# Eigenvalues by bisection: two counting passes and a straight line in place of the third pass

## The reference

```python
deg = jnp.sum(A, axis=0) + jnp.sum(A, axis=1) - jnp.diagonal(A)
d_inv_sqrt = jnp.where(deg > 0, jax.lax.rsqrt(deg), 0.0)
L_norm = d_inv_sqrt[:, None] * (jnp.diag(deg) - A) * d_inv_sqrt[None, :]
_, U = jnp.linalg.eigh(L_norm)
agg = jnp.einsum('mn,bnd->bmd', U.T, features)
h = jax.nn.relu(agg @ W1 + b1)
out = jnp.einsum('nm,bmd->bnd', U, h @ W2 + b2)
```

## Time and profile before

| | us |
|---|---|
| median of 3 runs (1450.54 to 1452.41) | 1451.95 |
| the profiled execution | 1448.35 |
| its span, first to last instruction | 1446.6 |
| mean granted TensorE clock in the span, of full speed | 0.895 |
| TensorE, VectorE, ScalarE, GpSimd busy | 1113.3, 834.3, 750.1, 544.8 |

### The profile page before, as it was taken

The page is one execution under the profiler, slowest core; times in us unless marked ns, Lnnn a source line. Parts: engine busy times, 40 slices in busy tenths (PEclk is TensorE's granted clock), DMA queues, the critical chain, the costliest instruction groups (busy, mean ns, idle before and its releaser), DMA issues. The chain is left out here.

```text
span 1446.6 us, 28045 instructions
## 1 busy us (share of the span) xinstructions
PE 1113.3 (77%) x6334; PEld 824.6 (57%) x6335; DVE 834.3 (58%) x3919; ACT 750.1 (52%) x2077; POOL 544.8 (38%) x843
## 2 busy tenths in 40 slices
PE   3444513729771999999967998999999689929996
PEld 2223312617661999999965664445444345529995
DVE  7777898977764433354548983444444578622221
ACT  4555534704340666666645775665655456515552
POOL 5666512500477772054437700000000006644554
PEclk9999955759855999999987999999999789959998
DMA  9500000000012333233321100000000002234330
GB/s 257 142 1 1 1 1 1 1 0 5 30 50 76 110 118 91 68 112 100 106 60 52 50 3 0 0 0 0 0 1 0 4 1 85 86 128 111 104 107 27
DMA packets 85701, 75.57 MB, mean 52 GB/s; under 512 B 13206, under 2 KB 74847, under 8 KB 85612
## 3 DMA queue, kind: packets, MB, share of 16 engines
q1 hardware_dynamic: 71788, 44.64, 11.2%
q0 software_dynamic: 13824, 29.98, 6.4%
HBM read 41.72 MB, written 33.37 MB: 52 GB/s over the span
## 5 line engine op out<-in xcount | busy, mean ns | idle before, releaser
L1220 POOL DMA_INDIRECT z<-spent,seats x64 | 63.5, 992 | 393.1 <-DVE spent L1341 375.7
L1687 ACT ACTIVATE c_H<-ps,c_b 128x128 f32<-128x128 f32 x576 | 157.0, 383 | 99.4 <-PE ps L1733 99.4
L2249 PE MATMUL ps<-BIG,spent 128*128 x364 | 156.0, 577 | 3.3 <-ACTq L2262 3.3
L1733 PE MATMUL ps<-ZS,c_w 128*128 128x128 f32 x1152 | 142.5, 277 | 2.7 <-ACT ZS L1676 1.6
L1719 PE MATMUL ps<-spent,c_H 128*128 x1152 | 140.3, 275 | 0.0
L1733 PEld LDWEIGHTS ps<-ZS,c_w 128*128 128x128 f32 x1152 | 136.0, 194 | 3.9 <-ACT ZS L1676 2.4
L1719 PEld LDWEIGHTS ps<-spent,c_H 128*128 128x128 f32 x1152 | 134.3, 192 | 0.0
L2249 PEld LDWEIGHTS ps<-BIG,spent 128*128 128x128 f32 x364 | 69.7, 192 | 84.5 <-issue 84.5
L2257 PE MATMUL ps<-e_hs,spent 128*128 128x512 f32 (+1 forms) x256 | 110.0, 572 | 0.0
L868 POOL DMA_INDIRECT z<-BIG,spots x64 | 63.7, 995 | 111.3 <-issue 102.3
L1587 POOL DMA_INDIRECT c_rows<-y,seats x64 | 60.7, 949 | 113.8 <-DMA y<-c_ys 59.4
(11 more groups left out here) (516 smaller groups left out, 2637.6 us busy)
## 6 DMA issues: line engine op xcount, KB each, us to landing
BIG<-z SPq DMA_DIRECT2D x72, 129.0 KB, 2.1
ZB<-z SPq DMA_DIRECT2D x144, 64.0 KB
y<-c_ys SPq DMA_DIRECT2D x72, 128.0 KB
spent<-in_L_ffn_W_dram SPq DMA_DIRECT2D x1, 2048.0 KB
spent<-in_L_ffn_W_dram SPq DMA_DIRECT2D x8, 256.0 KB
w_dn<-in_L_ffn_Wd_dram SPq DMA_DIRECT2D x8, 256.0 KB
z<-BIG,spots POOLq DMA_INDIRECT x128, 2.2
z<-j_padding SPq DMA_DIRECT2D x9, 129.0 KB, 2.7
```

Source lines behind the costliest of these rows:

```text
L1220: pool.indirect_dma_start(z, bass.IndirectOffsetOnAxis(ap=k.seats[:, 0, n:n + 1], axis=0), k.R[:, row(n), :], None, bounds_check=E * STRID ...
L1687: act.activation(H[u][:, c, h * P:(h + 1) * P], UP[u][c // 2][:, o:o + P], ACT.Gelu, bias=b1[u][h][:, c:c + 1]).then_inc(gelu, 1)
L1733: pe.matmul(UP[u][c // 2][:, o:o + P], w1[u][h][:, c * P:(c + 1) * P], ZT[u][:, h * P:(h + 1) * P], start=True, stop=True).then_inc(up, 1)
L2249: last = pe.matmul(view(k.ps[4 * u + j], wide, lanes), k.w_ihT[:, w, :], state(i, u, s, p, wide, lanes), start=True, stop=(s == 0))
```

## The change

`PASSES` becomes 2. The last pass keeps the number of points met (`hits`), and instead of a further pass VectorE takes, of both halves, the last two minors at the two neighbouring points between which the sign changes (`edge`, picked by comparing a row of indices with `at_k`, and summed to `edges`), scales them to at most one, and has TensorE exchange the halves. The products give the characteristic polynomial at both points (`ends`); the zero of the straight line through them, kept between the two points, goes into `nlo`.

With one pass less, `EARLY` becomes 3, so that groups 3 to 15 go beside the recurrence. All token statistics have to be done in two passes: six tiles after a sign instruction instead of four. VectorE's scales of the second part of the tokens move into the second pass.

```diff
-PASSES = 3
+PASSES = 2
...
-                        upto = min(first + 4, TILES)
+                        upto = min(first + 6, TILES)
...
+            pe.wait_ge(s_edges, 1)
+            pe.matmul(ps[5][:, 0:4], swap[:, :], edges[:, :], start=True, stop=True).then_inc(s_crossed, 1)
             for g in range(EARLY - 1, GROUPS):
                 tokens_turned(g)
...
-                if turn != 1:
+                if turn in (0, PASSES - 1):
...
-                link(stt(out=nlo, in0=hits, scalar=nwidth, in1=nlo, op0=ALU.mult, op1=ALU.add))
-            link(stt(out=nlo, in0=nwidth, scalar=0.5, in1=nlo, op0=ALU.mult, op1=ALU.add))
+                if turn < PASSES - 1:
+                    link(stt(out=nlo, in0=hits, scalar=nwidth, in1=nlo, op0=ALU.mult, op1=ALU.add))
+
+            link(ts_(at_k, hits, 1.0, float(SECT - 1), ALU.max, ALU.min))
+            for n in range(4):
+                got = link.put(stt(out=edge[:, n, :], in0=k.irow[:, 1 - n // 2:SECT + 1 - n // 2], scalar=at_k,
+                                   in1=minors[:, HALF - 1 + n % 2, :], op0=ALU.is_equal, op1=ALU.mult))
+            link.need(got)
+            link(dve.tensor_reduce(out=edges[:, :], in_=edge[:, :, :], axis=AX.X, op=ALU.add))
+            link.put(dve.tensor_reduce(out=most, in_=edges[:, :], axis=AX.X, op=ALU.max))
+            link(dve.tensor_reduce(out=fewest, in_=edges[:, :], axis=AX.X, op=ALU.min))
+            link(stt(out=most, in0=fewest, scalar=-1.0, in1=most, op0=ALU.mult, op1=ALU.max))
+            link(ts_(most, most, TINY, None, ALU.max))
+            link(dve.reciprocal(most, most))
+            ts_(edges[:, :], edges[:, :], most, None, ALU.mult).then_inc(s_edges, 1)
+            link.put(ts_(beyond, hits, 1.0, None, ALU.add))
+            dve.wait_ge(s_edges, 1)
+            dve.wait_ge(s_crossed, 1)
+            link(tt_(cross[:, :], edges[:, :], ps[5][:, 0:4], ALU.mult))
+            link(stt(out=ends[:, :], in0=cross[:, 0:4:2], scalar=coup2[:, 0:1], in1=cross[:, 1:4:2], op0=ALU.mult, op1=ALU.add))
+            link(tt_(most, ends[:, 0:1], ends[:, 1:2], ALU.subtract))
+            link(stt(out=most, in0=most, scalar=0.0, in1=most, op0=ALU.is_equal, op1=ALU.add))
+            link(dve.reciprocal(most, most))
+            link(stt(out=fewest, in0=ends[:, 0:1], scalar=most, in1=at_k, op0=ALU.mult, op1=ALU.add))
+            link(ts_(fewest, fewest, hits, beyond, ALU.max, ALU.min))
+            link(stt(out=nlo, in0=fewest, scalar=nwidth, in1=nlo, op0=ALU.mult, op1=ALU.add))
             link(ts_(where, nlo, 1 / STRETCH, None, ALU.mult))
```

More of the change, by code:

```diff
@@ L154, in spectrum @@
             sb(n, [P, SECT]) for n in ("step_t", "trial", "met", "ratio", "alike"))
+        edge, edges, cross, ends = sb("edge", [P, 4, SECT]), sb("edges", [P, 4]), sb("cross", [P, 4]), sb("ends", [P, 2])
+        at_k, most, fewest, beyond = (col(n) for n in "at_k most fewest beyond".split())
         order, fold, least, nlo, nwidth, hits, where = (
@@ L175, in spectrum @@
              "factor refined").split())
+        s_edges, s_crossed = sem("h_edges"), sem("h_crossed")
         s_x = [sem(f"h_x{q}") for q in range(4)]
```

## The result

The changed kernel took 1428.19 us (median of 4 runs, 1425.91 to 1429.24), the kernel before 1451.24 (4 runs, 1449.37 to 1452.41). The ratio is 0.9839, with a 95% interval of 0.9825 to 0.9853: 23.05 us faster. The forecast was 1428.2, from a gain of 23.7. One run of experiment 2 (1569.46 us, granted clock 0.80 in place of 0.89 to 0.90) was slow as a whole and is in neither its median nor its ratio.

A forecast was written before the change was run, and what follows sets the result against it. The prediction took VectorE's chain of dependent instructions as the bound in the eigensolver, with ScalarE and TensorE setting each pass's end. Gain 28.63 - 0.2 - 4.71 = 23.7 us from 1451.95 gave 1428.2 us, range 1424 to 1433.

The forecast's parts named there:

- the pass: Eigensolver's third counting pass: taking it out moves everything from alike on earlier by 28.63 us.
- the longer tail: VectorE from met to DD after the last pass: 6.05 us against 1.34, so 4.71 us more.
- the token work is covered: Token groups 2 to 15, queued behind the added matmul, cost nothing while the recurrence covers them; 12 us of cover.
- ScalarE's wider statistics: Six tiles instead of four between sign instructions in the two passes: net 0.2 us late.
- The hand-over to TensorE and back: The tail's exchange through TensorE: 0.68 us of idle on VectorE, ends 0.4 and 0.8.
- the four products: Four independent edge products, 64 wide, in VectorE's tail: 0.89 us, from overlap seen in the trace.
- The cover: Room between the end of the token groups and the vectors' norm, beside the recurrence: 12 us.
- The token work does not limit: Rival: with TensorE at half clock, token groups end 8.5 us after the norm; time 1436.7; chance 0.05.
- later stages give some back: Rival: four TensorE starts after rest each lose another 1.6 us to the clock, 6.4 in all; 1434.6; chance 0.05.
- the prediction's own sign of being wrong: Stretches after 465.7 us (old axis) growing longer by more than 2 us would show the forecast wrong.
- the slower rival: Rival: expert stage left at 1.2 GHz for a while by the shift; at 60 us, time 1458; chance 0.02.
- the pass was on the path: Rival denied here: something else holds the network's first stage, so removing the pass gains nothing; 1452; chance 0.02.

The follow-up runs named there:

- experiment 2: Kernel before with the straight line added but three passes kept, four tiles of statistics after a sign: 1454.65 us, ratio 1.003.
- first pair: First profiles of the kernel before and of the changed kernel, both unedited; their runs' medians were 1451.24 and 1428.19 us.
- experiments 6 and 7: Unedited repeats: 6 is the changed kernel again, 1427.38 us (ratio 0.9841); 7 is the kernel before again, 1450.94 us.
- experiment 1: Changed kernel without the straight line, the middle of the last interval taken instead: 1423.29 us, ratio 0.9815.
- experiments 3 and 4: Changed kernel with token statistics spread 9, 6, 4 and 9, 5, 0 (3: 1426.87 us), or second-pass exchange of ratio ahead of the token matmuls (4: 1423.97 us).
- Experiments 9 and 10: Changed kernel with the weight matmuls of token groups 3 to 14 made twice (9: 1429.51 us) or three times (10: 1425.53 us).
- experiment 5: Changed kernel with both the exchange ahead of the weight matmuls and statistics spread 9, 6, 4 and 9, 5, 0: 1425.37 us, ratio 0.9825.
- experiment 11: Changed kernel with exchange first, statistics spread, and unused 128-column TensorE matmuls (one, six, five) ahead of the graph layer: 1426.14 us, ratio 0.9823.

## Why the prediction was right

The mechanism was right: the pass comes off the path whole, the longer tail goes back on it, and the token work is covered. That the time came out at 1428.19 for 1428.2 is luck. The forecast took a gain of 23.7 us from 1451.95, and the runs gave one of 23.05 from 1451.24; the two errors cancel.

By steps, each in us of the start of the graph layer:

| step | forecast | first pair | experiments 6 and 7 |
|---|---|---|---|
| the pass | 28.63 | 28.63 | 28.75 |
| ScalarE's wider statistics | -0.2 | about +0.15 | +0.09 |
| a common start earlier, all of it ahead of the passes | 0 | +0.29 | -0.04 |
| the tail, 6.05 against 1.34 | -4.71 | -4.98 (6.32) | -4.80 (6.14) |
| set-up copies behind the tail | 0 | -0.27 | -0.01 |
| the recurrence up to the first graph matmul | 0 | -0.24 | -0.29 |
| sum | 23.7 | 23.58 | 23.70 |

The starts of the graph layer in experiments 7 and 6, from which the last sum comes:

```profile
323.17 3.75 PE L1119 MATMUL ps<-BDU,BIG 128*128 128x128 f32 x16 [2.37 <-PEq L2431]
```

```profile
299.47 3.75 PE L1148 MATMUL ps<-BDU,BIG 128*128 128x128 f32 x16 [2.39 <-PEq L2460]
```

The sums are closer than their terms: in the first pair errors of about 0.3 us stand on either side.

**The pass** came off whole because what follows `alike` is the same in either pass: `alike` to `met` is 2.26 us before and after. Its rows in the table are read from the kernel before, as in the forecast; what tests it are experiment 1 (28.67 us without the line) and experiment 2, which gives it back (28.89 with the line).

**ScalarE's statistics** had the wrong sign, and a size that hardly counts. `ratio` of the first pass ends 0.29 us earlier than before, before any edit can act; that is the table's third row, and it is gone in the second pair. The last sign of the first pass then held up VectorE by 0.59 us:

```profile
201.69 0.33 DVE L582 TENSOR_TENSOR h_changes<-BIG 128x320 bf16<-128x320 bf16 x1 [0.59 <-ACT BIG L326]
```

But `alike`, which before waited 0.46 us for TensorE at this point, now had no wait, so only 0.13 of it stayed (I put 0.3). The second `ZS` of the second pass, in the changed kernel and in the kernel before:

```profile
234.01 0.58 ACT L313 ACTIVATE ZS<-ps 128x512 f32<-128x512 f32 x1
```

```profile
234.44 0.58 ACT L310 ACTIVATE ZS<-ps 128x512 f32<-128x512 f32 x1
```

0.43 us earlier, or 0.14 beyond the common start, where I had 0.2 late. The chain itself (second `ZS`, token matmuls, exchange, `alike`) is as I read it; experiments 3 and 4 move it at either end.

**The tail** was 0.09 us too short in the forecast. In the first profile it takes 6.32 us, in the second 6.14, and 6.14 to 6.15 in the seven other versions with two passes and the line:

```profile
239.22 0.28 DVE L647 TENSOR_SCALAR h_met<-ps,h_least 128x64 f32<-128x64 f32 x1
...
244.22 0.22 DVE L672 SCALAR_TENSOR_TENSOR h_fewest<-h_ends,h_most,h_at_k 128x1 f32<-128x1 f32 x1
...
245.36 0.25 DVE L679 TENSOR_SCALAR h_DD<-h_DG,h_where 64x64 f32<-64x64 f32 x1 [0.17 <-DVEq L97]
```

The hand-over to TensorE and back was right (0.69 against 0.68), the four products nearly (0.94 us with their link, 0.89 forecast). The Trainium skill's rule ("VectorE: DVE Perf Modes", section "The TRN2 errata") that every small instruction pays its own latency would have made them 1.28; for independent neighbours the trace does not bear it out. Behind the exchange, `cross` to `DD` took 2.18 in the second profile, as forecast, and 2.35 in the first, where line 672 has 0.36 us in place of 0.22.

**The set-up copies** I had not looked at, as nothing in them is edited. The kernel before, and the changed kernel in its first profile:

```profile
270.02 0.25 DVE L651 TENSOR_SCALAR h_DD<-h_DG,h_where 64x64 f32<-64x64 f32 x1
...
270.67 0.32 DVE L653 COPY h_EE<-h_NE 64x63 f32<-64x63 f32 x1
271.02 0.17 DVE L654 COPY h_PV<-h_DD 64x2 f32<-64x2 f32 x1
```

```profile
245.93 0.35 DVE L680 TENSOR_SCALAR h_DD<-h_DG,h_where 64x64 f32<-64x64 f32 x1
...
246.67 0.39 DVE L682 COPY h_EE<-h_NE 64x63 f32<-64x63 f32 x1
247.09 0.29 DVE L683 COPY h_PV<-h_DD 64x2 f32<-64x2 f32 x1
```

The same instructions are 0.07 to 0.12 us longer. But in the second profile of the same kernel they are as before:

```profile
245.65 0.25 DVE L680 TENSOR_SCALAR h_DD<-h_DG,h_where 64x64 f32<-64x64 f32 x1
...
246.65 0.17 DVE L683 COPY h_PV<-h_DD 64x2 f32<-64x2 f32 x1
```

They are long, together with line 672, in the first profile and in experiment 2, and in no other of the 13 profiles. The unedited kernel shows both lengths, so these 0.45 us are no price of the line; their cause stays open.

**The recurrence** is longer in both pairs, by 0.24 and 0.29 us, where the forecast had nothing; why isn't shown.

**The cover** I put at 12 us, and it is 14.09 (13.04 in the second profile). The size came out near, for a reason that was not the right one: I added up TensorE's times of a group (1.76), while it is ScalarE that sets the pace at nearly the same figure (1.73). Experiments 9 and 10 were mis-sized by the same error, and by a group too many.

**The rivals.** The token work does not limit, and would from about 3.0 us a group. The prediction priced it at 8.5 us for a group of 3.24; at 3.12 (experiment 10) the root came 1.25 to 1.86 us late, so that price was too high. That later stages give some back was seen in the first profiled pair: from the first expert on it took 983.0 us in place of 980.9, which is past the prediction's own sign of being wrong (2 us). It fell with experiments 6 and 7, 979.9 and 980.2: the stage from the first graph matmul to the first expert takes 142.0 to 144.4 us with either kernel. The Trainium skill ("TensorE: Matmul & The Clock Gate", Part 1) says that the moment of the rise differs from run to run; these four profiles agree, with 2.4 us between the ends of this stage. The expert stage shows nothing of the slower rival: 282.9 us from its start to the gather before, 283.0 after. And the pass was on the path.

Of the versions that still draw the line and were run several times, the fastest is that of experiment 5, at 1425.37, some 2 us under the changed kernel in the same set of runs with intervals that overlap; its start of the graph layer, 2.3 us ahead of experiment 6, points the same way. Experiment 1, at 1423.29, is below it, but takes the middle of the interval as the eigenvalue.

## What to carry to other kernels

A chain of dependent instructions can be summed from the trace's own rows to a few per cent, if each kind of instruction is looked up at its width and each link and hand-over is counted: 6.05 us forecast, 6.14 and 6.32 measured, over 24 instructions. When two profiles differ by less or more than the sum, compare the stages one by one, and run the unedited kernels a second time, before the difference is put down to the change. That holds for single instructions too: 0.45 us here looked like a price of the line and was gone in the repeat. For the room under a cover, ask which engine sets the pace of the covered work; work added to another engine can be free up to that pace.

## What the runs showed of the hardware

The same program's stage of 142 us differed by 2.0 and 2.1 us between two profiles. More than half of that arose in 8 us in which the granted clock was 0.79 in one and 0.57 or 0.58 in the other, with 49 to 51 against 34 matmuls.

In two profiles out of 13 the same small VectorE instructions (three of the set-up, and line 672 where it is there) took 0.07 to 0.14 us more each; the second profile of one of these two kernels has them at their usual length.

With TensorE busy for 12.15 of the 17.25 us ahead of the graph layer the first 16 matmuls took 2.02 us; in the changed kernel, with 4.14 of 16.10 (below), 3.76; with two bursts of 2.93 and 2.50 us (experiment 11), 3.75.

```profile
284.00:300.10 16.10, 4.14 (x17) 3.07 (x18) 8.99 (x46) 0.30 (x1) 0.00 (x0) 0.50 0.00 0
```

Four independent products of 64 columns took 0.91 us together, where the first alone lasts 0.28 (240.09 to 240.37): these neighbours on VectorE overlap. Of two dependent ones, such as `met` and the reduction behind it, the second starts 0.03 to 0.04 us after the end of the first.
